# Two groups of eight heads in place of sixteen single heads, in the output and state step of a chunked recurrence on eight cores

## The chip, the cores and the metric

One Trainium2 chip, eight cores. Each core runs the same program on one of the eight batch rows (8192 tokens of 1024 channels), and the cores exchange nothing. The metric is the device time of the slowest core in microseconds.

## What is computed

A recurrent layer with a gate from a feed-forward network. The input is x of 8 x 8192 x 1024. It is normalised over its channels, mixed with the token before, and projected to k, v, r and g. k and v are normalised to unit length by head (16 heads of 64 channels). Then a state matrix of 64 x 64 for each head runs over the tokens:

```
def step(state, rkv):
    r_t, k_t, v_t = rkv
    pred = einsum('bhij,bhj->bhi', state, k_t)
    err = pred - v_t
    state = dec * state - et * (err[..., :, None] * k_t[..., None, :])
    n = maximum(sqrt(sum(state * state, axis=(-2, -1))), 1e-08)
    state = state * where(n > max_norm, max_norm / n, 1.0)
    wkv = einsum('bhij,bhj->bhi', state, r_t)
    return (state, wkv)
```

wkv is normalised over all tokens and channels of its head, projected with W_o and multiplied with silu(g). The feed-forward network (1024 to 3072 to 1024, integer weights times 1/127) works on the same normalised input. The output is x + s * silu(ffn).

## The kernel before

The program is written as one list of instructions for the five engines (`P.do`), with semaphores by hand. `P.do(..., inc=s)` lets the instruction raise the semaphore `s` when it is done, and puts a wait in front of it, on the same engine, until `s` has reached its present value. `P.wait(engine, s)` waits for the present value. `mark_free(tile, s)` notes at which value of `s` the PSUM bank of a tile is free, and `wait_free` waits for that. `P.drain` is a drain of one engine. `s_t` is raised by TensorE, `s_v` by VectorE, `s_s` by ScalarE, `s_g` by GpSimd's DMAs.

The tokens are cut into 64 chunks of 128. Chunks are worked in pairs: `phaseA` of both (normalising, four projections, the key and query products `mup` and `gkrm`, the transposed keys and queries `krfm`), one `dosolve` for both (the inverses of 32 x 32 triangles, on VectorE), then `phaseB` of one chunk after the other. After the 64 chunks comes a second part with the feed-forward network and the output projection, 32 blocks of 256 tokens, twice.

`phaseB` for one chunk does this in order. L671 and L674 scale the values. The loop of L685 to L714 solves for `ptl`, head by head, with TensorE and ScalarE in turn. L722 to L736 make sums of squares and `omb`. L739 to L799 work out the decay and norm factors `betcol` (one for each token and head) and `nbLb` (one for each head), with a way through DRAM and back. Then comes the loop over heads that the change touches (L809 to L839):

- L811 and L813: two matmuls into `pw`, 128 x 64 in float32. The first has the weights `krfm` of 64 rows, the second `gkrm` of 128 rows. They add up to the head's output before scaling.
- L818: VectorE scales `pw` by `betcol` into `wkvt` and writes the sum over the 64 channels to `statS` (the tile is named xntok in the trace). After a drain, L823 squares `wkvt` and writes the sum of the squares to `statQ`; its full output goes to a scratch tile.
- L831 and L833: two matmuls into `psg`, 64 x 64. The first has the weights `negibf` of 64 rows, the second the keys `ktokp` (named uni in the trace) of 128 rows. They give the new state before scaling.
- L837: VectorE scales `psg` by `nbLb` into `sigma`, the state of the head in bfloat16.

`pw` and `psg` are cuts of one PSUM bank, `pk2` (named pk in the trace), of 128 x 512 float32. All uses of this bank share one entry in the table behind `mark_free`, so L811 of a head waits for L837 of the head before. The heads don't depend on each other.

After the loop, L858 to L863 transpose `wkvt` two heads at a time (TensorE, then a copy by VectorE), and GpSimd's queue stores the result (L868). The next chunk's `phaseB` or `phaseA` begins on VectorE when that store has landed.

Of the kernel before, what the change touches and what calls it, by code (L numbers as in the profile page):

```python
# [13 lines left out]
OP = mybir.AluOpType  # L14
# [4 lines left out]
H = 16  # L19
D = 64  # L20
# [57 lines left out]
def build_nc(T, debug=False, upto=None, solvemode="", phb=""):  # L78
# [69 lines left out]
    negibf = sb("sb_negibf", [64, 64], BF16)  # L148
# [28 lines left out]
    scanbig = sb("scanbig", [128, 3072], BF16)  # L177
# [4 lines left out]
    ktokp = [uni2f[:, 0:C], uni2f[:, C:2 * C]]  # L182
# [18 lines left out]
    omb = sb("omb", [128, C], BF16)  # L201
# [67 lines left out]
    s_t = Sem(es, nc, "s_t")  # L269
    s_v = Sem(es, nc, "s_v")  # L270
# [3 lines left out]
    P = Prog()  # L274
# [384 lines left out]
    def phaseB(ch):  # L659
        par = ch % 2  # L660
# [21 lines left out]
        for h in range(H if "noptl" not in phb else 0):  # L682
# [5 lines left out]
            for jj in range(4):  # L688
# [4 lines left out]
                    start=False, stop=(jj == 0), skip_group_check=True,  # L693
# [112 lines left out]
        P.wait("tensor", s_v, v_omb)  # L806
        P.wait("tensor", s_v, v_betc)
        P.wait("tensor", s_v, v_nbl)
        for h in range(H if "nowkv" not in phb else 0):  # L809
            wait_free("tensor", id(pw))  # L810
            P.do("tensor", lambda e, h=h: e.matmul(  # L811
                pw[:], krfm[:, par, h, 1, :], sigma[:, D * h:D * (h + 1)], start=True, stop=False))
            P.do("tensor", lambda e, h=h: e.matmul(  # L813
                pw[:], gkrm[:, par * 2048 + 128 * h:par * 2048 + 128 * (h + 1)], omb[:, D * h:D * (h + 1)],
                start=False, stop=True), inc=s_t)
            P.wait("vector", s_t)
            acc1 = None if "noacc" in phb else 1
            P.do("vector", lambda e, h=h, ch=ch, acc1=acc1: e.tensor_scalar(  # L818
                wkvt[:, D * h:D * (h + 1)], pw[:], betcol[:, h:h + 1], 0.0, OP.mult, OP.add,
                accum_out=(statS[:, h, (ch % 8):(ch % 8) + 1] if acc1 else None)), inc=s_v)  # L820
            mark_free(id(pw), s_v)
            P.drain("vector")
            P.do("vector", lambda e, h=h, ch=ch, acc1=acc1: e.scalar_tensor_tensor(  # L823
                scanbig[:, 1024 + D * h:1024 + D * (h + 1)], wkvt[:, D * h:D * (h + 1)], 1.0,
                wkvt[:, D * h:D * (h + 1)],
                OP.mult, OP.mult, accum_out=(statQ[:, h, (ch % 8):(ch % 8) + 1] if acc1 else None)), inc=s_v)
            if "nosig" in phb:
                continue
            P.wait("tensor", s_v)
            wait_free("tensor", id(psg))  # L830
            P.do("tensor", lambda e, h=h: e.matmul(  # L831
                psg[:], negibf[:], sigma[:, D * h:D * (h + 1)], start=True, stop=False))
            P.do("tensor", lambda e, h=h: e.matmul(  # L833
                psg[:], ktokp[par][:, D * h:D * (h + 1)], omb[:, D * h:D * (h + 1)],
                start=False, stop=True), inc=s_t)
            P.wait("vector", s_t)
            P.do("vector", lambda e, h=h: e.tensor_scalar(  # L837
                sigma[:, D * h:D * (h + 1)], psg[:], nbLb[:, h:h + 1], 0.0, OP.mult, OP.add), inc=s_v)
            mark_free(id(psg), s_v)  # L839
        v_wkv = s_v.n  # L840
        if (ch % 8 == 7) or (ch == nch - 1):
            nsl = (ch % 8) + 1
# [105 lines left out]
    for nn in range(2):  # L948
        for k in range(CS):
# [6 lines left out]
            start=False, stop=True), inc=(s_t if nn == 1 else None))  # L956
# [17 lines left out]
    for phase in range(2):  # L974
# [26 lines left out]
        for mc in range(nmac):  # L1001
# [45 lines left out]
            for tb in range(2):  # L1047
                pdn = pjB
                wait_free("tensor", id(pjB))
                for nn in range(2):  # L1050
                    for ks in range(HSH):
# [3 lines left out]
                            start=(ks == 0), stop=(ks == HSH - 1)),  # L1055
                            inc=(s_t if (ks == HSH - 1 and nn == 1) else None))
# [9 lines left out]
                else:  # L1066
# [7 lines left out]
                    for nn in range(2):  # L1074
                        for k in range(CS):
# [6 lines left out]
                            inc=(s_t if nn == 1 else None))  # L1082
# [123 lines left out]
```

How the kernel before makes its waits and increments, by code:

```python
    def do(self, eng, fn, inc=None, k=1):  # L49
        def run(e, fn=fn, inc=inc, k=k):
            ins = fn(e)
            if inc is not None:
                ins.then_inc(inc.h, k)
        if inc is not None and k == 1 and inc.n > 0:
            self.recs.append((eng, lambda e, s=inc, v=inc.n: e.wait_ge(s.h, v)))
            self._snap()
        self.recs.append((eng, run))
        if inc is not None:
            inc.n += k
        self._snap()
# [1 line left out]
    def wait(self, eng, sem, val=None):  # L62
        v = sem.n if val is None else val
        if v > 0:
            self.recs.append((eng, lambda e, s=sem, v=v: e.wait_ge(s.h, v)))
            self._snap()
# [11 lines left out]
def build_nc(T, debug=False, upto=None, solvemode="", phb=""):  # L78
# [1026 lines left out]
    P.mark("p2", [s_ld, s_x0, s_x1, s_tr, s_g, s_t, s_v, s_s, s_o])
    if upto is not None:
        if isinstance(upto, int):
            cut = upto
            snap = dict(zip(P.sems, P.snaps[cut - 1])) if cut > 0 else {}
        else:
            cut, snap = P.marks[upto]
        P.recs = P.recs[:cut]
        for s, v in snap.items():
            P.recs.append(("sync", lambda e, s=s, v=v: e.wait_ge(s.h, v) if v > 0 else e.nop()))
    else:
        P.wait("sync", s_o)
        P.wait("sync", s_g)
```

## Time and profile before

| | us |
|---|---|
| time, median of 2 runs | 24416.74 (24402.82 to 24430.67) |
| time of the profiled execution | 24398.31 |
| span of its slowest core, core 6 | 24396.7 |
| spans of its eight cores | 24366.9 to 24396.7 |
| granted TensorE clock, mean of each core | 0.579 to 0.584 |

The profile shows one execution on its slowest core. Times are microseconds from the start of the span, unless marked ns. PE is TensorE's matmuls, PEld its weight loads, DVE is VectorE, ACT ScalarE, POOL GpSimd, SP SyncE; DVEq, PEq and so on are the sequencers of these engines. L12 is line 12 of the kernel. A clock of 0.50 is TensorE's level of 1.2 GHz, 1.00 that of 2.4 GHz. Matmul ends are modelled, so distances are best read from start to start.

### The profile page before, as it was taken

How to read it: one execution, taken by the hardware profiler on the slowest of the kernel's cores; microseconds unless marked ns; L12 is line 12 of the kernel's file. 1: busy time of each engine (PE TensorE's matmuls, PEld its weight loads, DVE VectorE, ACT ScalarE, POOL GpSimd, SP SyncE). 2: the span in 40 equal slices, each digit the busy share in tenths (PEclk: the TensorE clock that was granted, in tenths of full speed). 3: DMA queues.
4: the chain of work that ended last, by engine and by line, in shares of the span. 5: the costliest groups of instructions: out<-in, count | busy, mean ns of one | idle time of the engine just before them, and what ended most of it. 6: DMA issues, size and time to landing. Idle time of an engine off the chain costs nothing.

```text
span 24396.7 us, 201711 instructions; the slowest of 8 cores (24366.9 to 24396.7 us)
## 1 busy us (share of the span) xinstructions
PE 7643.1 (31%) x45771; PEld 4051.6 (17%) x45994; DVE 5793.6 (24%) x17712; ACT 3388.0 (14%) x12931; POOL 752.6 (3%) x1156
## 2 busy tenths in 40 slices
PE   1222222222222222222222222222222223774666
PEld 0111111111111111111111111111111112553333
DVE  2222222222222222222222222222222221111112
ACT  1111111111111111111111111111111111001000
POOL 0000000000000000000000000000000000000000
PEclk7555555555555555555555555555555556887888
DMA  1000000000000000000000000000000001102222
GB/s 36 7 7 7 7 7 7 7 7 7 7 7 7 7 7 7 7 7 7 6 7 7 7 7 6 7 7 7 7 7 7 7 6 53 34 33 79 70 70 64
DMA packets 298688, 408.20 MB, mean 17 GB/s; under 512 B 114907, under 2 KB 213629, under 8 KB 297602
## 3 DMA queue, kind: packets, MB, share of 16 engines
q1 hardware_dynamic: 162434, 260.39, 3.5%
q0 software_dynamic: 53248, 118.05, 2.7%
q10 hardware_dynamic: 81920, 16.84, 0.3%
q8 instruction: 491, 8.04, 0.1%
q14 instruction: 595, 4.87, 0.1%
HBM read 243.57 MB, written 134.22 MB: 15 GB/s over the span
## 4 chain that ended last, share of the span: by engine, by line
PE 32%; issue 23%; DVE 17%; ACT 11%; DMA 9%; ACTq 4%; DVEq 2%; POOL 1%; SPq 1%; POOLq 0%
PE pk L707 4%; ACT ysb L705 4%; ACT ptl L714 4%; PE pjA L1037 3%; PE pgB L1028 3%; DVE soltmp L621 3%; PE pjB L1052 3%; PE ppB L698 3%; PE pjA L479 2%; ACTq L442 2%; DVE xproj L464 2%; DVE solw L629 2%; PE pjB L479 2%; PE pgB L563 2%; DVEq L69 1%
## 5 line engine op out<-in xcount | busy, mean ns | idle before, releaser
L705 ACT CAST ysb<-ppB 32x64 bf16<-32x64 f32 x4096 | 833.5, 203 | 7828.1 <-PE ppB L689 5947.3
L725 DVE SCALAR_TENSOR_TENSOR scanbig<-ptl,dev 128x64 bf16<-128x64 bf16 x1024 | 231.0, 226 | 6970.1 <-ACT ptl L714 6785.5
L707 PE MATMUL pk<-ysb,thtiles 32*32 32x64 bf16 x4096 | 848.6, 207 | 2499.6 <-ACT ysb L705 2499.6
L479 PE MATMUL pjA<-WAR,xproj 128*128 128x512 bf16 x1922 | 578.2, 447 | 2321.8 <-DVEq L471 2284.0
L1028 PE MATMUL pgB<-xproj,WAR 128*128 128x256 bf16 x6144 | 918.9, 300 | 1176.0 <-DMA gkrm<-dpart_sc 773.5
L698 PE MATMUL ppB<-ptl,mup 32*32 32x64 bf16 (+2 forms) x3072 | 643.2, 209 | 1860.1 <-ACT ptl L714 1860.1
L685 PE MATMUL ppB<-sigma,krfm 64*128 64x64 bf16 x1024 | 212.6, 208 | 3161.9 <-DVE dev L674 2566.8
L714 ACT CAST ptl<-pk 32x64 bf16<-32x64 f32 x4096 | 832.5, 203 | 2502.6 <-PE pk L707 2502.6
L1042 DVE SCALAR_TENSOR_TENSOR scanbig<-pjA,omb 128x256 bf16<-128x256 f32 x768 | 326.4, 425 | 2403.9 <-PE pjA L1037 2243.3
L1037 PE MATMUL pjA<-xproj,WAR 128*128 128x256 bf16 x6144 | 884.1, 292 | 32.7 <-DVE scanbig L1042 5.9
L707 PEld LDWEIGHTS pk<-ysb,thtiles 32*32 32x32 bf16 x4096 | 391.3, 96 | 2949.6 <-issue 2949.6
L1028 PEld LDWEIGHTS pgB<-xproj,WAR 128*128 128x128 bf16 x6144 | 648.9, 107 | 1329.8 <-issue 1203.7
L1052 PE MATMUL pjB<-WAR,scanbig 128*128 128x512 bf16 x2976 | 702.0, 393 | 135.5 <-DVE scanbig L1042 80.6
L621 DVE TENSOR_TENSOR soltmp<-solw,soln 128x1 bf16<-128x1 bf16 (+30 forms) x992 | 711.3, 717 | 77.9 <-issue 4.8
L567 DVE SCALAR_TENSOR_TENSOR mup<-pgB,t_eta_b,sb_masksneg 128x128 bf16<-128x128 f32 x1024 | 359.5, 351 | 1535.4 <-PE pgB L563 1535.4
L1033 ACT ACTIVATE omb<-pgB 128x256 bf16<-128x256 f32 x768 | 295.0, 384 | 2760.7 <-PE pgB L1028 2739.3
L563 PE MATMUL pgB<-krfm 64*128 64x256 bf16 x1024 | 376.5, 368 | 951.7 <-DVE gkrm L570 881.3
L698 PEld LDWEIGHTS ppB<-ptl,mup 32*32 32x32 bf16 (+2 forms) x3072 | 300.5, 98 | 2203.4 <-issue 2203.4
L685 PEld LDWEIGHTS ppB<-sigma,krfm 64*128 64x128 bf16 x1024 | 103.8, 101 | 3276.5 <-issue 3276.5
L1037 PEld LDWEIGHTS pjA<-xproj,WAR 128*128 128x128 bf16 x6144 | 597.7, 104 | 284.0 <-issue 183.0
L479 PEld LDWEIGHTS pjA<-WAR,xproj 128*128 128x128 bf16 x2048 | 204.4, 110 | 2608.6 <-issue 2482.7
L831 PE MATMUL pk<-sigma,sb_negibf 64*64 64x64 bf16 x1024 | 234.8, 229 | 1182.2 <-DVE scanbig L823 1182.2
(201 smaller groups left out, 11362.2 us busy)
## 6 DMA issues: line engine op xcount, KB each, us to landing
xbuf<-x SPq DMA_DIRECT2D x128, 512.0 KB, 3.7
xproj<-xnfm_sc SPq DMA_DIRECT2D x128, 256.0 KB
dpart_sc<-uni POOLq DMA_DIRECT2D x64, 512.0 KB, 3.1
gkrm<-dpart_sc SPq DMA_DIRECT2D x64, 512.0 KB
out<-uni SPq DMA_DIRECT2D x64, 512.0 KB, 2.6
xnfm_sc<-xnfm POOLq DMA_DIRECT2D x128, 128.0 KB, 2.9
gsig_sc<-uni POOLq DMA_DIRECT2D x64, 256.0 KB, 2.3
wkvfm_sc<-scanbig POOLq DMA_DIRECT2D x128, 128.0 KB, 2.7
```

The lines of the kernel that those rows point to most:

```text
L442: P.do("scalar", lambda e, k=k: e.dma_start(out=xtr[k][:], in_=xntok[:, 128 * k:128 * (k + 1)], transpose=True), inc=s_tr, k=16)
L464: P.do("vector", lambda e, pi=pi, k=k, xsv=xsv: e.scalar_tensor_tensor(xproj[:, pi, k, :], mixtmp[:, k, :], tmc[:, pi, k:k + 1], xsv[:, k, :],
L479: P.do("tensor", lambda e, pi=pi, k=k, pst=pst, nn=nn: e.matmul(pst[:, 512 * nn:512 * (nn + 1)], xproj[:, pi, k, :], wlist[pi][:, k, 512 * ...
L563: P.do("tensor", lambda e, h=h: e.matmul(pg[:], krfm[:, par, h, 0, :], krfm[:, par, h, :, :].rearrange("p a t -> p (a t)"), start=True, st ...
L621: P.do("vector", lambda e, r=r, ns=ns: e.tensor_tensor(soltmp[:, 0:ns * ns].rearrange("p (c s) -> p c s", s=ns), solw[:].rearrange("p (s c ...
L698: P.do("tensor", lambda e, h=h, j=j: e.matmul(pp[32 * j:32 * (j + 1), :], mup[0:32 * j, par * 2048 + 128 * h + 32 * j:par * 2048 + 128 * h ...
L705: P.do("scalar", lambda e, j=j: e.copy(ysb[32 * j:32 * (j + 1), :], pp[32 * j:32 * (j + 1), :]), inc=s_s)
L707: P.do("tensor", lambda e, h=h, j=j, thp=thp: e.matmul(pp2[32 * j:32 * (j + 1), :], thp[32 * j:32 * (j + 1), 32 * h:32 * (h + 1)], ysb[32 ...
L714: P.do("scalar", lambda e, h=h, j=j: e.copy(ptl[32 * j:32 * (j + 1), D * h:D * (h + 1)], pp2[32 * j:32 * (j + 1), :]), inc=s_s)
L1028: P.do("tensor", lambda e, hs=hs, k=k: e.matmul(pg[:], fgh[:, k, 128 * hs:128 * (hs + 1)], p2xn[:, k, :], start=(k == 0), stop=(k == CS - ...
L1037: P.do("tensor", lambda e, hs=hs, k=k: e.matmul(pjA[:, 0:256], fuh[:, k, 128 * hs:128 * (hs + 1)], p2xn[:, k, :], start=(k == 0), stop=(k ...
L1052: P.do("tensor", lambda e, ks=ks, tb=tb, pdn=pdn, nn=nn: e.matmul(pdn[:, 512 * nn:512 * (nn + 1)], hfm[:, ks, 128 * tb:128 * (tb + 1)], fd ...
```

## The change

The loop over 16 heads becomes a loop over two groups of eight. Each group works in four blocks on the whole of `pk2`, of which each head has 64 of the 512 columns:

1. eight pairs of wkv matmuls, of which only the last raises `s_t`;
2. after one wait, eight scalings to `wkvt` with their sums; only the last raises `s_v`, and the bank is marked free at that value. Then one drain, and eight squarings;
3. the eight pairs of state matmuls, into rows 0 to 63 of the same bank. They wait until the bank is free, which is the last of the scalings. The former wait of TensorE for all that VectorE has issued is gone;
4. after one wait, eight scalings to `sigma`, with the bank marked free at the last.

The instructions of each head have the shapes and operands that they had, apart from the columns of the bank.

```
-        for h in range(H if "nowkv" not in phb else 0):
-            wait_free("tensor", id(pw))
-            P.do("tensor", lambda e, h=h: e.matmul(
-                pw[:], krfm[:, par, h, 1, :], sigma[:, D * h:D * (h + 1)], start=True, stop=False))
-            P.do("tensor", lambda e, h=h: e.matmul(
-                pw[:], gkrm[:, par * 2048 + 128 * h:par * 2048 + 128 * (h + 1)], omb[:, D * h:D * (h + 1)],
-                start=False, stop=True), inc=s_t)
+        acc1 = None if "noacc" in phb else 1
+        for hg in range(2 if "nowkv" not in phb else 0):
+            wait_free("tensor", id(pk2))
+            for hh in range(8):
+                h = 8 * hg + hh
+                P.do("tensor", lambda e, h=h, hh=hh: e.matmul(
+                    pk2[:, 64 * hh:64 * (hh + 1)], krfm[:, par, h, 1, :],
+                    sigma[:, D * h:D * (h + 1)], start=True, stop=False))
+                P.do("tensor", lambda e, h=h, hh=hh: e.matmul(
+                    pk2[:, 64 * hh:64 * (hh + 1)],
+                    gkrm[:, par * 2048 + 128 * h:par * 2048 + 128 * (h + 1)],
+                    omb[:, D * h:D * (h + 1)],
+                    start=False, stop=True), inc=(s_t if hh == 7 else None))
             P.wait("vector", s_t)
-            P.do("vector", lambda e, h=h, ch=ch, acc1=acc1: e.tensor_scalar(
-                wkvt[:, D * h:D * (h + 1)], pw[:], betcol[:, h:h + 1], 0.0, OP.mult, OP.add,
-                accum_out=(statS[:, h, (ch % 8):(ch % 8) + 1] if acc1 else None)), inc=s_v)
-            mark_free(id(pw), s_v)
-            P.drain("vector")
-            P.do("vector", lambda e, h=h, ch=ch, acc1=acc1: e.scalar_tensor_tensor(
-                ...
-                OP.mult, OP.mult, accum_out=(statQ[:, h, (ch % 8):(ch % 8) + 1] if acc1 else None)), inc=s_v)
+            for hh in range(8):
+                h = 8 * hg + hh
+                P.do("vector", lambda e, h=h, hh=hh, ch=ch, acc1=acc1: e.tensor_scalar(
+                    wkvt[:, D * h:D * (h + 1)], pk2[:, 64 * hh:64 * (hh + 1)], betcol[:, h:h + 1],
+                    0.0, OP.mult, OP.add,
+                    accum_out=(statS[:, h, (ch % 8):(ch % 8) + 1] if acc1 else None)),
+                    inc=(s_v if hh == 7 else None))
+            mark_free(id(pk2), s_v)
+            P.drain("vector")
+            for hh in range(8):
+                h = 8 * hg + hh
+                P.do("vector", lambda e, h=h, ch=ch, acc1=acc1: e.scalar_tensor_tensor(
+                    ...
+                    inc=(s_v if hh == 7 else None))
             if "nosig" in phb:
                 continue
-            P.wait("tensor", s_v)
-            wait_free("tensor", id(psg))
-            P.do("tensor", lambda e, h=h: e.matmul(
-                psg[:], negibf[:], sigma[:, D * h:D * (h + 1)], start=True, stop=False))
-            P.do("tensor", lambda e, h=h: e.matmul(
-                psg[:], ktokp[par][:, D * h:D * (h + 1)], omb[:, D * h:D * (h + 1)],
-                start=False, stop=True), inc=s_t)
+            wait_free("tensor", id(pk2))
+            for hh in range(8):
+                h = 8 * hg + hh
+                P.do("tensor", lambda e, h=h, hh=hh: e.matmul(
+                    pk2[0:64, 64 * hh:64 * (hh + 1)], negibf[:],
+                    sigma[:, D * h:D * (h + 1)], start=True, stop=False))
+                P.do("tensor", lambda e, h=h, hh=hh: e.matmul(
+                    pk2[0:64, 64 * hh:64 * (hh + 1)], ktokp[par][:, D * h:D * (h + 1)],
+                    omb[:, D * h:D * (h + 1)],
+                    start=False, stop=True), inc=(s_t if hh == 7 else None))
             P.wait("vector", s_t)
-            P.do("vector", lambda e, h=h: e.tensor_scalar(
-                sigma[:, D * h:D * (h + 1)], psg[:], nbLb[:, h:h + 1], 0.0, OP.mult, OP.add), inc=s_v)
-            mark_free(id(psg), s_v)
+            for hh in range(8):
+                h = 8 * hg + hh
+                P.do("vector", lambda e, h=h, hh=hh: e.tensor_scalar(
+                    sigma[:, D * h:D * (h + 1)], pk2[0:64, 64 * hh:64 * (hh + 1)], nbLb[:, h:h + 1],
+                    0.0, OP.mult, OP.add), inc=(s_v if hh == 7 else None))
+            mark_free(id(pk2), s_v)
         v_wkv = s_v.n
```

## Rows read from the trace of the kernel before

**Rows 1.** The page: span, busy time of each engine, chain by engine.

```profile
span 24396.7 us, 201711 instructions; the slowest of 8 cores (24366.9 to 24396.7 us)
...
PE 7643.1 (31%) x45771; PEld 4051.6 (17%) x45994; DVE 5793.6 (24%) x17712; ACT 3388.0 (14%) x12931; POOL 752.6 (3%) x1156
...
PE 32%; issue 23%; DVE 17%; ACT 11%; DMA 9%; ACTq 4%; DVEq 2%; POOL 1%; SPq 1%; POOLq 0%
```

**Rows 2.** Chain of waits, one head's first matmul and the next head's: start, us, what.

```profile
5574.93 0.21 PE pk L811
...
5577.46 0.21 PE pk L811
```

**Rows 3.** Timeline, second head and the third's L813: start, us, engine, operation, idle before.

```profile
5574.93 0.21 PE L811 MATMUL pk<-sigma,krfm 64*128 64x64 bf16 x1 [0.60 <-DVE sigma L837]
...
5575.08 0.23 PE L813 MATMUL pk<-omb,gkrm 128*128 128x64 bf16 x1
5575.50 0.28 DVE L818 TENSOR_SCALAR_CACHE_REDUCE xntok<-pk,betcol 128x64 bf16<-128x64 f32 x1 [0.71 <-PE pk L813]
5575.71 0.08 DVE L818 DVE_READ_ACCUMULATOR xntok<-pk,betcol 128x1 f32 x1
5575.95 0.23 DVE L823 SCALAR_TENSOR_TENSOR scanbig<-xntok 128x64 bf16<-128x64 bf16 x1 [0.16 <-DVE xntok L818]
5576.11 0.08 DVE L823 DVE_READ_ACCUMULATOR scanbig<-xntok 128x1 f32 x1
...
5576.44 0.23 PE L831 MATMUL pk<-sigma,sb_negibf 64*64 64x64 bf16 x1 [1.13 <-DVE scanbig L823]
...
5576.60 0.26 PE L833 MATMUL pk<-omb,uni 128*64 128x64 bf16 x1
5577.04 0.28 DVE L837 TENSOR_SCALAR sigma<-pk,nbLb 64x64 bf16<-64x64 f32 x1 [0.85 <-PE pk L833]
...
5577.60 0.24 PE L813 MATMUL pk<-omb,gkrm 128*128 128x64 bf16 x1
```

**Rows 4.** Timeline, the loop's first instructions and the first after it.

```profile
5572.05 0.21 PE L811 MATMUL pk<-sigma,krfm 64*128 64x64 bf16 x1 [0.59 <-DVE nbLb L799]
...
5572.20 0.23 PE L813 MATMUL pk<-omb,gkrm 128*128 128x64 bf16 x1
5572.97 0.28 DVE L818 TENSOR_SCALAR_CACHE_REDUCE xntok<-pk,betcol 128x64 bf16<-128x64 f32 x1 [1.17 <-PE pk L813]
...
5613.23 0.29 PE L858 MATMUL ptw<-sb_identbf,xntok 128*64 128x128 bf16 x1 [0.71 <-DVE sigma L837]
```

**Rows 5.** Views of single lines: count, ns min/median/max, first and last start.

```profile
L811 PE MATMUL pk<-sigma,krfm x1024: 206/209/210, 566.9 to 20244.6; 64*128 64x64 bf16 x171
...
L858 PE MATMUL ptw<-sb_identbf,xntok x512: 283/287/288, 607.9 to 20254.7; 128*64 128x128 bf16 x171
```

**Rows 6.** Stretches: window, length, busy time of each engine, clock, DMA.

```profile
5572.00:5613.10 41.10, 12.79 (x64) 7.30 (x64) 12.84 (x80) 0.00 (x0) 0.00 (x0) 0.50 0.00 1
```

**Rows 7.** Timeline, the projections: L479 and L482, clock rising on the way.

```profile
5210.19 3.19 PE L479 MATMUL pjA<-WAR,xproj 128*128 128x512 bf16 x7 [32.17 <-DVEq L471]
...
5213.31 0.60 PE L482 MATMUL pjA<-WAR,sb_onesb_r 1*128 1x512 bf16 x1
...
5213.85 1.90 PE L479 MATMUL pjA<-WAR,xproj 128*128 128x512 bf16 x8
```

**Rows 8.** Timeline, four transposes of phase A side by side.

```profile
5237.48 0.60 PE L551 MATMUL ptw<-sb_identbf,uni 128*64 128x128 bf16 x4 [0.87 <-ACT krfm L555]
```

**Rows 9.** Line L464 and its timeline: VectorE operations with nothing between.

```profile
L464 DVE SCALAR_TENSOR_TENSOR xproj<-scanbig,tmc,xnfm x2048: 343/344/354, 198.5 to 19757.7; 128x128 bf16<-128x128 bf16 x187
...
5200.95 8.23 DVE L464 SCALAR_TENSOR_TENSOR xproj<-scanbig,tmc,xnfm 128x128 bf16<-128x128 bf16 x31
```

**Rows 10.** Timeline, two of sixteen L725, with an accumulator and a drain behind each.

```profile
5553.20 0.23 DVE L725 SCALAR_TENSOR_TENSOR scanbig<-ptl,dev 128x64 bf16<-128x64 bf16 x1
...
5553.51 0.23 DVE L725 SCALAR_TENSOR_TENSOR scanbig<-ptl,dev 128x64 bf16<-128x64 bf16 x1
```

More of the change, by code:

```diff
@@ L808, in phaseB @@
         P.wait("tensor", s_v, v_nbl)
-        for h in range(H if "nowkv" not in phb else 0):
-            wait_free("tensor", id(pw))
-            P.do("tensor", lambda e, h=h: e.matmul(
-                pw[:], krfm[:, par, h, 1, :], sigma[:, D * h:D * (h + 1)], start=True, stop=False))
-            P.do("tensor", lambda e, h=h: e.matmul(
-                pw[:], gkrm[:, par * 2048 + 128 * h:par * 2048 + 128 * (h + 1)], omb[:, D * h:D * (h + 1)],
-                start=False, stop=True), inc=s_t)
-            P.wait("vector", s_t)
-            acc1 = None if "noacc" in phb else 1
-            P.do("vector", lambda e, h=h, ch=ch, acc1=acc1: e.tensor_scalar(
-                wkvt[:, D * h:D * (h + 1)], pw[:], betcol[:, h:h + 1], 0.0, OP.mult, OP.add,
-                accum_out=(statS[:, h, (ch % 8):(ch % 8) + 1] if acc1 else None)), inc=s_v)
-            mark_free(id(pw), s_v)
-            P.drain("vector")
-            P.do("vector", lambda e, h=h, ch=ch, acc1=acc1: e.scalar_tensor_tensor(
-                scanbig[:, 1024 + D * h:1024 + D * (h + 1)], wkvt[:, D * h:D * (h + 1)], 1.0,
-                wkvt[:, D * h:D * (h + 1)],
-                OP.mult, OP.mult, accum_out=(statQ[:, h, (ch % 8):(ch % 8) + 1] if acc1 else None)), inc=s_v)
@@ new lines, in phaseB @@
+        acc1 = None if "noacc" in phb else 1
[11 more added lines that the diff above has]
+                    start=False, stop=True), inc=(s_t if hh == 7 else None))
+            P.wait("vector", s_t)
+            for hh in range(8):
[6 more added lines that the diff above has]
+            mark_free(id(pk2), s_v)
+            P.drain("vector")
+            for hh in range(8):
+                h = 8 * hg + hh
+                P.do("vector", lambda e, h=h, ch=ch, acc1=acc1: e.scalar_tensor_tensor(
+                    scanbig[:, 1024 + D * h:1024 + D * (h + 1)], wkvt[:, D * h:D * (h + 1)], 1.0,
+                    wkvt[:, D * h:D * (h + 1)],
+                    OP.mult, OP.mult, accum_out=(statQ[:, h, (ch % 8):(ch % 8) + 1] if acc1 else None)),
+                    inc=(s_v if hh == 7 else None))
```

## The prediction

> **What bounds the kernel now.** I read the page first. No engine is full: TensorE is busy for 31% of the span, VectorE for 24%, ScalarE for 14% [rows 1]. The chain that ended last is spread over TensorE, "issue", VectorE, ScalarE and DMA in turn, so this is a kernel of latencies: one engine waits for the other, and nothing overlaps [rows 1]. A handshake that disappears is paid back in full if it lies on that chain.
>
> Next the chain of waits inside one chunk. One head's L811 is on it at 5574.93 us, the next head's at 5577.46, 2.53 us later, and between them it holds every other instruction of the head [rows 2]. The timeline of the same head shows what the 2.53 us are made of [rows 3]. L811 to L813 start 0.15 apart; L813 to L818 0.42; L818 to L823 0.45; L823 to L831 0.49; L831 to L833 0.16; L833 to L837 0.44; L837 to the next L811 0.42 (0.15+0.42+0.45+0.49+0.16+0.44+0.42 = 2.53).
>
> The whole loop runs from 5572.05 to the first transposing L858 at 5613.23, 41.18 us [rows 4]; in the first chunk it is 566.9 to 607.9, 41.0 [rows 5]. It runs 64 times (x1024 heads) [rows 5], so it holds 64 x 41.18 = 2636 us, 10.8% of the span. All of the change happens here, between 566.9 and 20254.7 us [rows 5]. The stretches view gives the loop a granted clock of 0.50, the 1.2 GHz level, with TensorE busy for 12.79 of 41.10 us [rows 6].
>
> **The change, part by part.** Two groups of eight heads take the place of sixteen heads. Matmuls and VectorE operations are the same in number and shape. What goes is handshakes: four crossings per head (TensorE to VectorE and back, twice) become four per group. I sum one group from first L811 to the next group's first L811.
>
> *Crossings that stay.* L813 to L818, 0.42. Last L833 to L837, 0.44. L837 back to TensorE, 0.42. The new crossing, last L818 to L831, is not shown before: L831 used to wait for the square L823. L823 starts 0.49 before L831, its accumulator read ends 0.24 after its start, so 0.25 is the way to TensorE; L818's read ends 0.29 after its start, hence 0.29 + 0.25 = 0.54 [rows 3]. Sum of the four: 1.82 us.
>
> *Train of 16 wkv matmuls.* It alternates L811 (64 rows of weights) and L813 (128 rows). The step L811 to L813 is 0.145 us (0.15 in the second head, 0.14 in the third) [rows 2, 3]. 64 columns at 1.2 GHz are 0.053, so changing the row size costs about 0.09. The step back from 128 rows to 64 is not shown. The nearest is L482, whose weights have one row, inside the dense projections: at the lower clock it starts at 5213.31 and the next L479 (128 rows) at 5213.85, 0.54 later, where seven L479 before it are (3.19-0.60)/6 = 0.43 apart, 512 columns at 1.2 GHz; so 0.11 extra [rows 7]. 0.053 + 0.11 gives 0.165. Train: 8 steps of 0.145 and 7 of 0.165 = 2.32 us. Lower bound: no cost of changing, the spacing of the four L551, (0.60-0.29)/3 = 0.10 to 0.11 (one transpose of that shape has 0.287 [rows 5], and the four fill 0.60 [rows 8]); 128 columns at 1.2 GHz are 0.107, 15 x 0.107 = 1.60. Upper bound: no overlap at all, the modelled durations 0.21 and 0.23 in turn [rows 3], 15 x 0.22 = 3.3.
>
> *Train of 16 sigma matmuls.* The step L831 to L833 is 0.16 [rows 3]; with 0.165 for the step back: 8 x 0.16 + 7 x 0.165 = 2.43. Lower bound again 1.60; upper (0.23 and 0.26 in turn [rows 3]) 15 x 0.245 = 3.7.
>
> The Trainium skill speaks against this part: "TensorEngine Tiling (Array Packing)", section Key Properties, says that changing the tiling mode drains TensorE, which both trains do at every matmul. The steps of 0.145 and 0.16 against 0.107 agree with such a cost, and without the rule the two trains would be 1.60 each instead of 2.32 and 2.43, 1.55 us less per group.
>
> *Eight L818.* Between two of them there is now neither drain nor wait. The operation is 0.28 us, its accumulator read begins 0.21 after its start and ends at 0.29 [rows 3]. For operations with nothing between them the nearest row is L464: 31 of 0.344 us fill 8.23 us, (8.23-0.344)/30 = 0.263 apart, an overlap of 0.08 [rows 9]. So a step lies between 0.21 and 0.31 (L725, sixteen with drain and accumulator, start 0.31 apart [rows 10]). I take 0.25: 7 x 0.25 = 1.75.
>
> *Eight L823.* They follow after a drain, 0.45 behind the last L818. The sigma train no longer waits for them, only for the last L818, so they run beside it: 0.45 + 7 x 0.22 + 0.24 = 2.23 us after the last L818, against 0.54 + 2.43 + 0.44 = 3.41 for the train. They cost nothing; even at 0.31 a step they need 2.86. They would come on the path if the train had its lower bound (2.58) and L823 its upper, by 0.3 us.
>
> *Eight L837.* 0.28 us each [rows 3], with the same overlap 0.20 a step: 7 x 0.20 = 1.4. Lower bound 0.16, the distance at which L823 of the same width lets its accumulator read start [rows 3]. Upper bound 0.28, no overlap.
>
> Group: 1.82 + 2.32 + 1.75 + 2.43 + 1.40 = 9.72 us. Chunk: 2 x 9.72, plus what the present loop has beyond its steady heads: the first head is 0.35 longer (L818 starts 0.77 behind L813 instead of 0.42 [rows 3, 4]) and the way from the last L837 to L858 is 0.11 longer than that back to L811 (TensorE idle 0.71 against 0.60 [rows 3, 4]). Both stay: 19.44 + 0.46 = 19.90 us, instead of 41.18. Gain 21.28 us, x 64 = 1362 us.
>
> Nothing else moves: SP, GpSimd and ScalarE have no part in the loop, and behind it TensorE's L858 starts as early as the last L837 lets it, with VectorE's copies, GpSimd's store and the next chunk queued behind in the order they have now. The gain goes straight through. Against the profiled execution: 24396.7 - 1362 = 23035 us of span, 1.6 us more as time, 23036. The median of the runs shown is 24416.7, 18 above the profiled one, within 0.1%; I set 23045 between them, 5.6% below before.
>
> **Rivals.**
> *A, changing the row size costs nothing in a train* (the pair's 0.145 would be the start of a pair after a pause, not its pace). Trains of 1.60; L823 is then still hidden. Group 9.72 - 1.55 = 8.17, 128 groups: -198, 22840. For it: no row shows a train that alternates. Against: L482, inside a dense train, has its 0.11. Chance 0.13.
>
> *B, VectorE gains nothing from lying side by side.* Steps as long as with drains: L818 0.31, L837 0.28: + 7 x 0.06 + 7 x 0.08 = 0.98 a group, +125 us, 23165. For it: L725. Against: L464's overlap, without an accumulator though. Chance 0.17. The Trainium skill, "VectorE: DVE Perf Modes", section "The DRAIN you can't avoid", says exactly this: eight copies took the same time with a semaphore behind each and behind the last alone. L464's spacing below its duration disagrees with it here.
>
> *C, TensorE runs the alternating train without overlap*, 3.3 and 3.7 long: + 0.98 + 1.27 = 2.25 a group, +288, 23330. For it: weights of the next matmul may not be loaded while the array changes its rows. Against: both steps seen. Chance 0.14.
>
> *D, slower than before.* The mechanism would be the same change of rows, at a price no row shows: in each of 30 steps of a group TensorE would empty and refill. To eat the gain of 10.64 us a group a step would have to grow by 0.355, from 0.158 to 0.51 us. At 0.60, 30 x 0.44 = 13.3 a group, 2.6 us net loss, x 128 = 330: 24730. The longest way that a matmul takes here even with a handshake is 0.42 to 0.44. Chance 0.01. Between, with steps of 0.42, the gain would be 10.64 - 7.9 = 2.8 a group, 355 us, 1.5%: chance 0.02.
>
> *E, the clock goes up.* TensorE's work is in trains of 16 matmuls now instead of pairs. The projections went from 0.427 us a matmul to 0.21 inside one unbroken train [rows 7]; the loop's trains are broken by VectorE steps of 2 us. At 2.4 GHz a step falls by 0.027: 30 x 0.027 x 128 = 104 us less, 22940. Chance 0.05.
>
> **How the numbers follow.** My own sum 0.48, A 0.13, B 0.17, C 0.14, E 0.05, D and its weaker form 0.03. With every part at its lower bound a group loses 0.72 + 0.83 + 7 x 0.04 + 7 x 0.04 = 2.11 us, 270 in all: 22775. With every part at its upper bound (B and C together) it gains 3.23 us, 413 in all: 23460. The range leaves out only the last corner of the second: 22780 to 23420. Over 2% (what a measurement of this kernel can surely tell from no change; 488 us) faster: all but D, 0.97, taken as 0.96; within 2% 0.03; slower 0.01.
>
> **What would show it.** In the profile of the changed kernel: two groups a chunk, L811's first to L858's first near 19.9 us; in each 16 wkv matmuls within 2.3 to 2.6 us, alternating steps near 0.15 and 0.165; eight L818 spaced 0.25; the sigma train starting 0.5 us behind the last L818 while the squares run; eight L837 spaced 0.20. Wrong would be: squares that end after the sigma train; a granted clock above 0.50 in the loop; a later stretch (L858, the solve, the solution loop) that has become longer; or a saving per chunk in the loop that does not come back times 64 in the span.

## The result and the profile after

The changed kernel takes 23068.3 us (median of 9 runs, 23011.8 to 23298.8) against 24434.9 before (8 runs): a ratio of 0.9433, 95% interval 0.9417 to 0.9448, 5.7% faster. The longest of the nine executions, in which cores 0 to 3 ran at a lower clock than the others, is left out of the ratio. The prediction was 23045 us.

The profiled execution has a span of 23066.7 us, 1330 less than before. This is the page of the changed kernel: span, busy times, chain by engine.

```profile
span 23066.7 us, 191950 instructions; the slowest of 8 cores (22839.2 to 23066.7 us)
...
PE 7581.3 (33%) x45994; PEld 4036.1 (17%) x45994; DVE 5560.3 (24%) x17712; ACT 3388.0 (15%) x12931; POOL 750.3 (3%) x1156
...
PE 33%; issue 21%; DVE 17%; ACT 11%; DMA 9%; ACTq 4%; DVEq 2%; POOL 1%; SPq 1%; POOLq 0%
```

TensorE's and ScalarE's busy times are nearly those of [rows 1]. VectorE's is 233 us shorter although it has the same operations: its neighbours now overlap by up to 0.08 us, and what overlaps is counted once. About 9,800 instructions are gone, waits and, for 896 of them, drains. The work is the same and the pauses are shorter.

The timeline of one chunk's loop on core 7 (start, us, engine, operation, idle before) shows the four blocks of the first group, and where the second group and the transposes begin:

```profile
5244.95 0.21 PE L814 MATMUL pk<-sigma,krfm 64*128 64x64 bf16 x1 [0.59 <-DVE nbLb L799]
...
5245.09 0.24 PE L817 MATMUL pk<-omb,gkrm 128*128 128x64 bf16 x1
...
5245.26 0.23 PE L814 MATMUL pk<-sigma,krfm 64*128 64x64 bf16 x1
...
5245.42 0.24 PE L817 MATMUL pk<-omb,gkrm 128*128 128x64 bf16 x1
...
5247.42 0.24 PE L817 MATMUL pk<-omb,gkrm 128*128 128x64 bf16 x1
5247.78 0.28 DVE L825 TENSOR_SCALAR_CACHE_REDUCE xntok<-pk,betcol 128x64 bf16<-128x64 f32 x1 [3.08 <-PE pk L817]
...
5249.22 0.28 DVE L825 TENSOR_SCALAR_CACHE_REDUCE xntok<-pk,betcol 128x64 bf16<-128x64 f32 x1
...
5249.65 0.23 PE L844 MATMUL pk<-sigma,sb_negibf 64*64 64x64 bf16 x1 [2.00 <-DVE xntok L825]
...
5249.81 0.26 PE L847 MATMUL pk<-omb,uni 128*64 128x64 bf16 x1
...
5250.00 0.26 PE L844 MATMUL pk<-sigma,sb_negibf 64*64 64x64 bf16 x1
...
5250.19 0.26 PE L847 MATMUL pk<-omb,uni 128*64 128x64 bf16 x1
...
5250.63 0.22 DVE L834 SCALAR_TENSOR_TENSOR scanbig<-xntok 128x64 bf16<-128x64 bf16 x1
...
5252.47 0.26 PE L847 MATMUL pk<-omb,uni 128*64 128x64 bf16 x1
5252.84 1.62 DVE L854 TENSOR_SCALAR sigma<-pk,nbLb 64x64 bf16<-64x64 f32 x8 [1.99 <-PE pk L847]
...
5254.61 0.21 PE L814 MATMUL pk<-sigma,krfm 64*128 64x64 bf16 x1 [1.88 <-DVE sigma L854]
...
5264.38 0.29 PE L876 MATMUL ptw<-sb_identbf,xntok 128*64 128x128 bf16 x1 [1.99 <-DVE sigma L854]
```

One group takes 5254.61 - 5244.95 = 9.66 us, the loop 5264.38 - 5244.95 = 19.43 us, where it took 41.18 [rows 4]. The last of the squares (L834, 5250.63) starts almost two microseconds before the last matmul of the state train: they are hidden. The stretches view gives the same clock as in [rows 6], 0.50:

```profile
5244.90:5264.30 19.40, 11.57 (x64) 7.34 (x64) 9.20 (x80) 0.00 (x0) 0.00 (x0) 0.50 0.00 1
```

41.18 - 19.43 = 21.75 us, times 64 is 1392 us. The slowest core became only 1330 us faster, the others up to 1530 (core 2: 24366.9 to 22839.2). The cores end within 30 us of each other in the profiled execution of before and 228 apart in this one. The change did not make that difference: in the other executions of the kernel before, timed beside the experiments, the cores end 59 to 274 us apart. What tells the cores apart had no place in the prediction; e6 below is about it.

### The profile page after: what moved, and what is told of

The parts are those of the page before. It is cut to its first block, busy times and chain, and to the rows that moved or that the text cites. A ratio compares the mean times of both kernels' runs of the same rounds, so it can differ in the third digit from the quotient of the medians.

```text
span 23066.7 us, 191950 instructions; the slowest of 8 cores (22839.2 to 23066.7 us)
## 1 busy us (share of the span) xinstructions
PE 7581.3 (33%) x45994; PEld 4036.1 (17%) x45994; DVE 5560.3 (24%) x17712; ACT 3388.0 (15%) x12931; POOL 750.3 (3%) x1156
## 4 chain that ended last, share of the span: by engine, by line
PE 33%; issue 21%; DVE 17%; ACT 11%; DMA 9%; ACTq 4%; DVEq 2%; POOL 1%; SPq 1%; POOLq 0%
PE pk L707 4%; ACT ysb L705 4%; ACT ptl L714 4%; PE pjA L1055 4%; PE pgB L1046 3%; DVE soltmp L621 3%; PE pjB L1070 3%; PE ppB L698 3%; PE pjA L479 3%; ACTq L442 2%; DVE xproj L464 2%; DVE solw L629 2%; PE pjB L479 2%; PE pgB L563 2%; DVEq L69 2%
## 5 line engine op out<-in xcount | busy, mean ns | idle before, releaser
L725 DVE SCALAR_TENSOR_TENSOR scanbig<-ptl,dev 128x64 bf16<-128x64 bf16 x1024 | 230.9, 226 | 6965.1 <-ACT ptl L714 6888.6
L479 PE MATMUL pjA<-WAR,xproj 128*128 128x512 bf16 x2048 | 611.4, 452 | 2286.8 <-DVEq L471 2150.8
L685 PE MATMUL ppB<-sigma,krfm 64*128 64x64 bf16 x1024 | 212.7, 208 | 3168.1 <-DVE dev L674 2573.2
L714 ACT CAST ptl<-pk 32x64 bf16<-32x64 f32 x4096 | 832.6, 203 | 2499.0 <-PE pk L707 2499.0
L685 PEld LDWEIGHTS ppB<-sigma,krfm 64*128 64x128 bf16 x1024 | 103.8, 101 | 3282.5 <-issue 3282.5
L479 PEld LDWEIGHTS pjA<-WAR,xproj 128*128 128x128 bf16 x2048 | 205.3, 110 | 2604.2 <-issue 2483.8
L551 PE MATMUL ptw<-sb_identbf,uni 128*64 128x128 bf16 x2048 | 309.0, 306 | 837.1 <-DVEq L537 445.0
```

Of the source, the lines that this page charges most:

```text
L479: P.do("tensor", lambda e, pi=pi, k=k, pst=pst, nn=nn: e.matmul(pst[:, 512 * nn:512 * (nn + 1)], xproj[:, pi, k, :], wlist[pi][:, k, 512 * ...
L714: P.do("scalar", lambda e, h=h, j=j: e.copy(ptl[32 * j:32 * (j + 1), D * h:D * (h + 1)], pp2[32 * j:32 * (j + 1), :]), inc=s_s)
```

## The experiments

All were timed beside the kernel before (its medians 24437 to 24445 us), to which the ratios refer. The mean length of a chunk's loop is from its first wkv matmul to the first transpose, averaged over the 64 chunks of a core; it differs by at most 0.1 us between cores. The cuts of code show the lines that matter; `...` stands for lines left out.

| | loop, us | time, us | ratio to before |
|---|---|---|---|
| before | 41.1 | 24434.9 | 1 |
| e1, single heads, state matmuls don't wait for the square | 32.9 | 23869.5 | 0.976 (0.972 to 0.980) |
| e3b, groups of two | 24.25 | 23372.5 | 0.957 (0.952 to 0.961) |
| e3, groups of four | 21.03 | 23156.6 | 0.947 (0.943 to 0.951) |
| the changed kernel, groups of eight | 19.45 | 23068.3 | 0.943 (0.942 to 0.945) |
| e2, groups of eight, squares on the path | 22.4 | 23219.6 | 0.948 (0.943 to 0.954) |
| e4, groups of eight, each head raises | 25.8 | 23468.8 | 0.960 (0.958 to 0.963) |
| e5, groups of eight, rows sorted | 12.46 | 22663.4 | 0.926 (0.923 to 0.930) |

### e1: the removed wait alone

```
-            P.wait("tensor", s_v)
             wait_free("tensor", id(psg))
```

> The kernel before, with one line taken out: the state matmuls no longer wait for everything VectorE has issued, so they wait only for the scaling L818 (through the bank) and the square L823 runs beside them. My theory (two causes: the squares leave the path, and the crossings between engines are shared by eight heads): a head falls from 2.53 to 2.02 to 2.13 us, since L818 to L831 falls from 0.94 to 0.43 to 0.54; that is 410 to 520 us less, about 23970 us, a ratio near 0.981 to before. Rival 1 (nearly all of the gain is that wait): near 23100. Rival 2 (the squares don't matter, only the grouping does): no change, 24430.

It measured 23869.5 us, 569 less than before (24438.6). One head, from the timeline of e1 (its L830 and L832 are the state matmuls, L836 the scaling of the state):

```profile
5462.73 0.21 PE L811 MATMUL pk<-sigma,krfm 64*128 64x64 bf16 x1 [0.60 <-DVE sigma L836]
...
5463.30 0.28 DVE L818 TENSOR_SCALAR_CACHE_REDUCE xntok<-pk,betcol 128x64 bf16<-128x64 f32 x1 [0.71 <-PE pk L813]
...
5463.74 0.23 PE L830 MATMUL pk<-sigma,sb_negibf 64*64 64x64 bf16 x1 [0.63 <-DVE xntok L818]
5463.75 0.22 DVE L823 SCALAR_TENSOR_TENSOR scanbig<-xntok 128x64 bf16<-128x64 bf16 x1 [0.16 <-DVE xntok L818]
...
5464.34 0.28 DVE L836 TENSOR_SCALAR sigma<-pk,nbLb 64x64 bf16<-64x64 f32 x1 [0.35 <-PE pk L832]
...
5464.76 0.21 PE L811 MATMUL pk<-sigma,krfm 64*128 64x64 bf16 x1 [0.60 <-DVE sigma L836]
```

A head is 2.03 us instead of 2.53. L818 to the state matmul is 0.44 instead of 0.94, and the square starts at the same time as the matmul. So deleting one line, without any grouping, is worth 8.2 us a chunk, 64 x 8.2 = 525 us: 38% of what the whole change takes from the loop. Both rivals are out, "nearly all is the wait" as well as "only the grouping". The other 44 us are less than the interval of the ratio leaves open (0.972 to 0.980, about 100 us to either side).

### e2: the removed wait put back into the groups

```
+            P.wait("tensor", s_v)
             wait_free("tensor", id(pk2))
```

> The changed kernel with the removed wait put back: the state train of a group waits for the eight squares too. My theory: last scaling to first state matmul grows from 0.43 to 0.38 + 7 x 0.147 + 0.23 + 0.25 = 1.9 us, 1.46 us a group, 187 us in all, about 23255. Rival 1 (the wait is nearly all of the gain): back towards 24400. Rival 2: no change, 23070.

It measured 23219.6 us, 151 more than the changed kernel, and the loop 22.4 us instead of 19.45, 2.96 more (expected 2 x 1.46 = 2.92). Once grouped, the wait costs the loop 64 x 2.96 = 189 us, a third of what it costs with single heads: eight squares in a row put 1.48 us on the path, 0.185 each, where a single one puts 0.5 there. Neither rival came.

### e3 and e3b: the size of a group

```
-        for hg in range(2 if "nowkv" not in phb else 0):
+        for hg in range(4 if "nowkv" not in phb else 0):      # e3b: 8
-            for hh in range(8):
+            for hh in range(4):                                # e3b: 2
```

> The changed kernel with four groups of four heads. From the rows of the changed kernel a group of n heads costs 1.59 of crossings + (2n-1) x 0.166 + (n-1) x 0.206 + (2n-1) x 0.19 + (n-1) x 0.192: 9.7 us for n = 8, 5.28 for n = 4. Four groups 21.1 instead of 19.4 us a chunk, 110 us more, about 23180. The rival that only whole-bank use matters, or that the gain has nothing to do with the number of crossings, gives 23070.

> The changed kernel with eight groups of two heads. By the same sum a group costs 3.05 us, eight 24.4 instead of 19.4 us, 320 us more, about 23390. If crossings overlap when groups are short, less; if the number of crossings is not the cause, 23070.

They measured 23156.6 and 23372.5 us, with loops of 21.03 and 24.25 against expected 21.1 and 24.4. The sum over crossings and steps, read from groups of eight, holds within 0.15 us a chunk for four and for two. From single heads with the short wait (32.9) the groups of two bring 8.6 us, four another 3.2, eight another 1.6. Almost two thirds of what groups of eight bring is there with two heads.

### e4: the same crossings, but every head raises its semaphore

```
-                    start=False, stop=True), inc=(s_t if hh == 7 else None))
+                    start=False, stop=True), inc=s_t)
```

and likewise in the three VectorE blocks. `P.do` puts a wait on the same engine in front of each raising instruction.

> The changed kernel in which every head's last instruction of each block raises the semaphore again, so that each has the wait for the one before on its own engine; the crossings stay four a group. Theory 1 (an engine's own wait costs the full duration of the instruction before): L825 step from 0.206 to about 0.35, L854 from 0.192 to about 0.33, the wkv and state pairs by at most 0.05 each; 2.0 to 2.7 us a group, 250 to 350 us in all, 23320 to 23420. Theory 2 (only crossings cost): 23070.

It measured 23468.8 us, 400 above the changed kernel and 50 above the upper end of theory 1. The timeline of e4 on core 2, first two of the scalings to `wkvt`, then the eight scalings to `sigma` in one row:

```profile
5345.01 0.28 DVE L825 TENSOR_SCALAR_CACHE_REDUCE xntok<-pk,betcol 128x64 bf16<-128x64 f32 x1 [3.34 <-PE pk L817]
...
5345.42 0.28 DVE L825 TENSOR_SCALAR_CACHE_REDUCE xntok<-pk,betcol 128x64 bf16<-128x64 f32 x1
...
5351.60 2.96 DVE L854 TENSOR_SCALAR sigma<-pk,nbLb 64x64 bf16<-64x64 f32 x8 [0.28 <-PE pk L847]
```

A step of L825 is 0.41 us instead of 0.206, one of L854 (2.96-0.28)/7 = 0.38 instead of (1.62-0.28)/7 = 0.19. An operation that raises the semaphore and waits for the one before on its own engine costs 0.2 us more than one that does neither, though no other engine is involved. No run has the wait without the raising, so the 0.2 us belong to both together. This is 2 x 7 x (0.205 + 0.19) = 5.5 of the 6.4 us by which the loop grew; TensorE's pairs in the wkv train, 0.36 instead of 0.33, and the crossings into VectorE, 0.40 and 0.41 instead of 0.36 and 0.37, make up the rest. With single heads this wait shows little, because the operation before on the same engine is long done: the sum of e3 gives 1.59 + 0.166 + 0.19 = 1.95 us for one head without it, and a head of e1, which has it, takes 2.03. So what goes when single heads are grouped is crossings; the wait has to be taken out along with them, or part of the gain is lost again.

### e5: the rows sorted

```
-                    sigma[:, D * h:D * (h + 1)], start=True, stop=False))
+                    sigma[:, D * h:D * (h + 1)], start=(hh == 0), stop=False, skip_group_check=True))
+            for hh in range(8):
+                h = 8 * hg + hh
                 P.do("tensor", lambda e, h=h, hh=hh: e.matmul(
```

> The changed kernel with the matmuls of a train sorted by the rows of their weights: eight of 64 rows, then eight of 128 rows, in both trains. Only the first of a bank has the start flag, the others find it cleared. If changing the row size is what makes a step 0.166 and 0.19 instead of 0.107: the trains fall from 2.47 and 2.82 to about 1.65, 2.0 us a group, 256 us less, about 22810. If the steps come from the weight loads or the adding up in the same columns, not from the rows: 23070.

It measured 22663.4 us, 405 below the changed kernel, more than expected. Timeline of e5 on core 4, one group:

```profile
5110.56 0.58 PE L814 MATMUL pk<-sigma,krfm 64*128 64x64 bf16 x8 [0.59 <-DVE nbLb L799]
...
5111.07 0.61 PE L819 MATMUL pk<-omb,gkrm 128*128 128x64 bf16 x8
5111.81 0.28 DVE L827 TENSOR_SCALAR_CACHE_REDUCE xntok<-pk,betcol 128x64 bf16<-128x64 f32 x1 [1.50 <-PE pk L819]
...
5113.68 0.60 PE L846 MATMUL pk<-sigma,sb_negibf 64*64 64x64 bf16 x8 [2.00 <-DVE xntok L827]
...
5114.80 0.08 DVE L836 DVE_READ_ACCUMULATOR scanbig<-xntok 128x1 f32 x1
5114.95 1.62 DVE L858 TENSOR_SCALAR sigma<-pk,nbLb 64x64 bf16<-64x64 f32 x8
...
5116.72 0.58 PE L814 MATMUL pk<-sigma,krfm 64*128 64x64 bf16 x8 [1.88 <-DVE sigma L858]
```

Eight L814 fill 0.58 us where one is 0.21: (0.58-0.21)/7 = 0.053 a step, the 64 columns at 1.2 GHz and nothing else. In the changed kernel a step is 0.166 in this train and 0.19 in the state train. Each change of the row size thus costs 0.11 to 0.14 us. The other differences between the two trains don't explain it. Weights are loaded for each of the eight in both kernels. In the changed kernel the step from L814 to L817, which adds up in the same columns, is as long as that from L817 to L814, which goes to other columns and to a matmul with the start flag (5245.09, 5245.26, 5245.42; in the state train 5249.81, 5250.00, 5250.19). And the eight L728 of e9, all with the start flag and with weights of their own, go at 0.053 a step (row in e9 below).

From first to last start the wkv train is now 5111.07 + 7 x 0.053 - 5110.56 = 0.88 us instead of 2.47, and the state train 0.92 instead of 2.82: 2 x 3.49 = 7.0 us a chunk, which is all that the loop lost (19.45 to 12.46). The squares are only just hidden now: L858 starts 0.07 us after the last square's read ends. The Trainium skill ("TensorEngine Tiling (Array Packing)", Key Properties) says that a change of the tiling mode drains TensorE; these runs agree with it and give it a price.

### e6: the factors without the way through DRAM

```
-            P.do("gpsimd", lambda e: e.dma_start(out=dr["rowb"][0, :], in_=betT[:, 127:128]), inc=s_g, k=16)
-            P.wait("gpsimd", s_g)
-            P.do("gpsimd", lambda e: e.dma_start(out=glrow[:], in_=dr["rowb"][0:1, :]), inc=s_g, k=16)
-            ...
+            P.do("vector", lambda e: e.tensor_scalar(
+                glsq[:], identf[0:16, 0:16], betT[:, 127:128], None, OP.mult), inc=s_v)
+            ...
+            P.do("tensor", lambda e: e.matmul(pbl[:], masksneg[0:16, 64:128], glsq[:], start=True, stop=True), inc=s_t)
```

> The changed kernel in which the factors nbLb are spread by a matmul with a diagonal instead of two transfers through DRAM (L792, L794), whose way from L785 to L797 takes 4.4 us a chunk on most cores and 6.2 on cores 6 and 7 of the changed kernel's profile. If this way is what tells the cores apart: 3.6 to 5.5 us less a chunk, 230 to 350 less in all, and the spread of the cores at the end of the 64 chunks (18772 to 18904 before) falls below 40 us. If the cores differ for another reason the saving is the same on all of them and the spread stays near 130.

It measured 22759.0 us, 309 less than the changed kernel (ratio to before 0.931, 0.928 to 0.934). The waits view of the changed kernel has a reason why its cores differ: what TensorE waited for the loaded row (us in total, times, longest), first on core 0, then on core 7.

```profile
PE pk L797 <- DMA glrow<-rowb: 290.9, 64, 5.1
...
PE pk L797 <- DMA glrow<-rowb: 414.0, 64, 7.2
```

The same two transfers of 16 numbers cost 123 us more in 64 chunks on core 7. Cores 0 to 5 have 287 to 291 us, cores 6 and 7 411 and 414. The same view of the kernel before has 341.5, 400.5, 428.3 and 366.2 us on cores 0, 2, 5 and 6, so the difference was there before the change. The last transpose of the last chunk starts, in the changed kernel on cores 0, 4, 6 and 7 and then in e6 on cores 0, 2, 4, 6 and 7, at these times (view of the transposing line; the last number before the semicolon):

```profile
L876 PE MATMUL ptw<-sb_identbf,xntok x512: 283/287/288, 584.1 to 18786.3; 128*64 128x128 bf16 x171
L876 PE MATMUL ptw<-sb_identbf,xntok x512: 283/287/288, 586.9 to 18814.4; 128*64 128x128 bf16 x171
L876 PE MATMUL ptw<-sb_identbf,xntok x512: 283/287/287, 584.1 to 18920.2; 128*64 128x128 bf16 x171
L876 PE MATMUL ptw<-sb_identbf,xntok x512: 283/287/287, 587.7 to 18919.1; 128*64 128x128 bf16 x171
```

```profile
L875 PE MATMUL ptw<-sb_identbf,xntok x512: 283/287/288, 580.7 to 18578.9; 128*64 128x128 bf16 x171
L875 PE MATMUL ptw<-sb_identbf,xntok x512: 283/287/287, 580.4 to 18547.9; 128*64 128x128 bf16 x171
L875 PE MATMUL ptw<-sb_identbf,xntok x512: 283/287/288, 580.6 to 18549.0; 128*64 128x128 bf16 x171
L875 PE MATMUL ptw<-sb_identbf,xntok x512: 283/287/287, 580.0 to 18559.1; 128*64 128x128 bf16 x171
L875 PE MATMUL ptw<-sb_identbf,xntok x512: 283/287/287, 583.3 to 18554.0; 128*64 128x128 bf16 x171
```

Over all eight cores 134 us lie between them in the first and 34 in the second; in the kernel before it was 95 (20235.2 to 20330.3). So this way is most of what tells the cores apart at the end of the 64 chunks. They still end 226 us apart in e6 (22611.5 to 22837.8), and that comes from the feed-forward part: from L875's last start to the end it takes 4041 us on core 0, at a granted clock of 0.84, and 4289 on core 4, at 0.75. In the changed kernel's profile the two parts are of about one size: of the 228 us between cores 2 and 7, 116 are there at the end of the chunks (18802.9 against 18919.1) and 111 come behind it. Why the transfers are slower on some pairs of cores, and on other pairs in other runs, is not settled; no run here tries it.

### e7, e8 and e9: versions that go further

e7 works on all sixteen heads in the two pairs of banks `pjA` and `pjB`, which are idle here, with sorted rows, one matmul of 512 columns with `negibf` in place of eight, and wide VectorE operations:

```
+            P.do("tensor", lambda e, hg=hg: e.matmul(
+                pjB[0:64, 512 * hg:512 * (hg + 1)], negibf[:],
+                sigma[:, 512 * hg:512 * (hg + 1)], start=True, stop=False, skip_group_check=True))
...
+        P.do("vector", lambda e: e.tensor_tensor(
+            sigma[:].rearrange("p (h d) -> p h d", d=D), pjB[0:64, :].rearrange("p (h d) -> p h d", d=D),
+            nbLb[:].unsqueeze(2).to_broadcast([64, H, D]), OP.mult), inc=s_v)
```

> The loop for all sixteen heads at once, in the two pairs of banks that are idle here: rows sorted, one matmul of 512 columns with negibf in place of eight, VectorE scales 512 and 1024 columns in one operation with a broadcast factor, sums by reductions, and the transposes wait for wkvt alone. Expected: TensorE done 6.0 us after the start, sigma written by 7.7, squares and reductions by 9.7, with the transposes beginning beside them: loop and transposes 17 us instead of 27.4, 640 us less, about 22430. If VectorE's wide operations on PSUM cost what the sixteen small ones did (16 x 0.2), only the crossings are gained: 22800.

It measured 22280.8 us (ratio 0.910, 0.908 to 0.913), 150 below the expected 22430: TensorE needs 3.9 us for its 50 matmuls instead of 6.0, because sorted steps are 0.053 and not 0.107, and loop and transposes take 15.0 us instead of 17. TensorE's last matmul of the loop ends at 5063.55; what ends last is now VectorE, whose first copy of a transpose has to wait for the sums (timeline of e7):

```profile
5059.37 0.58 PE L814 MATMUL pjA<-sigma,krfm 64*128 64x64 bf16 x8 [0.70 <-DVE nbLb L799]
...
5063.73 1.22 DVE L849 TENSOR_TENSOR sigma<-pjB,nbLb 64x1024 bf16<-64x1024 f32 x1
5064.87 0.67 DVE L854 TENSOR_TENSOR soltmp<-xntok 128x1024 bf16<-128x1024 bf16 x1
5065.69 1.22 DVE L856 TENSOR_REDUCE uni<-soltmp 128x16 f32<-128x1024 bf16 x1
5067.01 0.23 DVE L881 COPY scanbig<-ptw 128x128 bf16<-128x128 bf16 x1
```

e8 adds e6 and does the sixteen transposes in two groups of eight.

```
+                P.do("tensor", lambda e, hh=hh, q=q: e.transpose(
+                    ptw[0:64, 128 * q:128 * (q + 1)], wkvt[:, D * hh:D * (hh + 1)], identbf[:]))
...
+            P.do("vector", lambda e, hq=hq: e.tensor_copy(
+                wkvfmb[:, 4 * hq:4 * (hq + 1), :].rearrange("p a t -> p (a t)"), ptw[:, 0:512]), inc=s_v)
```

> The wide loop of e7, the factors without DRAM as in e6, and the sixteen transposes in two groups of eight in place of eight pairs. e7 at 22281 us, less 309 as in e6, less 64 x 4 us (six of eight round trips of 0.95 us go, the groups' own work of 0.8 us each stays): about 21710. If the ways through DRAM and the transposes are hidden behind what e7 left on VectorE, less is gained: 22000.

It measured 21605.7 us, ratio 0.885 (0.881 to 0.889): 675 less than e7, where 309 + 260 were expected. So neither part is hidden; where the other 106 us come from was not looked into.

e9 is e8 with the same idea in the loop L685 to L714, which this change did not touch: each of its eight steps for eight heads at once, one ScalarE copy of 32 x 512 in place of eight of 32 x 64, two groups taking turns.

```
+            for g in range(2):
+                P.wait("scalar", s_t, tv[g])
+                P.do("scalar", lambda e, g=g, j=j: e.copy(
+                    ybig[32 * j:32 * (j + 1), 512 * g:512 * (g + 1)], gpp[g][32 * j:32 * (j + 1), :]), inc=s_s)
```

> e8, and the same idea applied to the loop L685 to L714, which takes 105.7 us of every chunk: each of its eight steps is done for eight heads in one bank, with one ScalarE copy of 32 x 512 in place of eight of 32 x 64, in two groups that take turns. A step of one group: eight matmuls of about 0.1, crossing 0.36, a copy of about 0.6, crossing 0.4; with two groups interleaved about 2.3 us; eight steps 18.5, the opening matmuls 4 to 5: 24 us instead of 105.7, 82 x 64 = 5230 less, about 16480. If this kernel's time is bound by the number of crossings on the chain, as the theory says, this is where most of it is; if the chain has other work behind it that then shows (ScalarE, VectorE, DMA), much less is gained: above 18000.

It measured 15676.6 us, ratio 0.642 (0.639 to 0.645). The stretch from the first matmul to the end of the last copy is 13.1 us, where it is 107.2 before and in e8 (64 x 94.1 = 6022 us, 5929 measured from e8 to e9). The stretches view of e9, and a row of its timeline:

```profile
3260.10:3273.30 13.20, 10.30 (x192) 8.08 (x192) 0.00 (x0) 9.23 (x16) 0.00 (x0) 0.50 0.01 2
...
3263.24 0.58 PE L728 MATMUL pjB<-soltmp,thtiles 32*32 32x64 bf16 x8 [0.34 <-ACT soltmp L721]
```

This is 11 us shorter than expected: the steps of its trains were taken as 0.1, and eight L728 fill 0.58 us, (0.58-0.21)/7 = 0.053 a step. TensorE is busy for 10.3 and ScalarE for 9.2 of 13.2 us: most of the waits of this loop are gone.

## Why the prediction was right, point by point

**Where the time lies.** "The gain goes straight through" held: the loop lost 21.75 us a chunk, predicted 21.28, and 1330 of the 1392 us came back in the span of the slowest core. Of the missing 62, 48 are the way through DRAM, for which TensorE waited 366.2 us on core 6 before and 414.0 on core 7 now. It was 428.3 us on core 5 before, so this is how that way varies and not an effect of the change.

**The sum of a group**, 9.72 predicted and 9.66 measured, is made of errors that cancel, 0.54 us too little for the trains and 0.60 too much for the rest. The crossings, steps and trains were the right terms; that their sum came within 0.06 us is luck:

| part | predicted | measured |
|---|---|---|
| wkv train | 2.32 | 2.47 |
| L817 to L825 | 0.42 | 0.36 |
| seven steps of L825 | 1.75 | 1.44 |
| last L825 to L844 | 0.54 | 0.43 |
| state train | 2.43 | 2.82 |
| L847 to L854 | 0.44 | 0.37 |
| seven steps of L854 | 1.40 | 1.34 |
| last L854 to L814 | 0.42 | 0.43 |

*The trains* were mis-sized by 0.54 us a group. The step from 64 to 128 rows was read off a pair that starts after a pause; in a train each of the two steps is 0.166, and 0.19 in the state train. The lower bound was wrong as well: 0.107 came from transposes of 128 columns, while matmuls of 64 columns go at 0.053 (e5). So rival A's price, 22840, was no bound: the kernel without changes of rows is e5, 22663.

*VectorE's steps* were taken too long for L825: its next operation starts as soon as the accumulator read starts, 0.206. Rival B is out with it. With it falls, for this kernel, what "VectorE: DVE Perf Modes" (the Trainium skill, "The DRAIN you can't avoid") says, that a semaphore behind each operation costs nothing: e4, where each operation also waits for the one before, has the two at 0.2 us an operation.

*The crossings* into VectorE came out 0.06 to 0.07 shorter each, and that from L825 to TensorE 0.11. In e4, where the instruction behind the crossing has the wait on its own engine, the crossings into VectorE are 0.40 and 0.41 again. So 0.04 to 0.05 of what I had read as the crossing goes with that wait.

*The squares* are hidden, as forecast: they end 1.6 us after the last L825, the train and its crossing need 3.6.

*The first head's extra 0.35 us* did not stay: L817 to the first L825 is 0.36 in the first group too. It was added as fixed and was not.

**The cause as I named it**, "what goes is handshakes", was too narrow. By the experiments the 21.6 us a chunk are 8.2 for the squares that leave the path (e1), which needs no grouping, and 13.4 for the grouping. Taken in the other order they are 18.7 for the grouping (41.1 to 22.4, e2) and 3.0 for the squares: the two causes overlap, since grouping also shares the crossings of the squares. And with four crossings a group but a wait in front of each head's instruction 6.4 us are lost again (e4).

**The rivals A, C, D and E** did not come: the steps of the trains are 0.166 and 0.19 us, not 0.107 (A), 0.22 and 0.245 (C) or 0.42 and more (D), and the clock stayed at 0.50 (E).

**What was not in it:** the cores. The saving in time (1367 us) equals the sum (1362) by chance in part. The loop gave (41.1 - 19.45) x 64 = 1386 us on every core. What the slowest core makes of it depends on its way through DRAM and on its clock in the feed-forward part, and both differ between cores and runs.

## What to carry to other kernels

In a kernel whose engines are all idle two thirds of the time, count for each loop how often the chain changes engine and how often an instruction waits for its own engine: here 0.4 us for a crossing, and 0.2 us for an operation that waits for the one right before it and raises the semaphore. Independent heads can share both, and most of it comes with the first doubling (e3b). Before regrouping, look for a wait for everything where a wait for one buffer does (e1: one line, 2.4%), sort matmuls by the rows of their weights (e5: 1.7%), and begin with the longest such loop rather than the nearest: the untouched one here was worth four times this change (e8 to e9: 5929 us).

## What the runs showed of the hardware

- Changing between weights of 64 and 128 rows from one matmul to the next costs 0.11 to 0.14 us at a granted clock of 0.50. Without it, matmuls of 64 columns follow each other in 0.053 us, even where each has new weights of 128 columns (L819 in e5).
- A VectorE operation of 64 columns follows the one before in 0.147 us (bfloat16 from SBUF, with accumulator), 0.19 to 0.206 us (float32 from PSUM); where each raises a semaphore and waits for the one before in 0.34 us and 0.38 to 0.41 us (e4).
- A way of 16 numbers (64 bytes) to DRAM and back cost TensorE a wait of 4.5 us on some cores and 6.5 us on others in the same run (290.9 us in 64 chunks on core 0, 414.0 on core 7), the two cores of a pair alike (289.3 on core 1, 410.7 on core 6).
- In the wkv and state trains of e5 only the first matmul into a bank has the start flag. The other heads of the bank, in columns of their own, come out without anything of what these columns held before.
